# Order of the first and second scores in the second attention of a hybrid block on one Trainium2 core

## The reference, cut to what matters

```python
x = x + linear_attention(layernorm(x))
x = x + experts(layernorm(x))
x = x + softmax_attention(layernorm(x))      # 16 heads of 8 channels
x = x + experts(layernorm(x))

# softmax_attention, the stage of the change
scores = einsum('bhqd,bhkd->bhqk', q, k) / sqrt(8)
attn = softmax(scores, axis=-1)
out = einsum('bhqk,bhkd->bhqd', attn, v)     # then the output projection
```

## Time and profile before

| | us |
|---|---|
| median of 3 runs | 548.59 (548.36 to 549.55) |
| the profiled execution | 548.98 |
| its span in the trace | 547.3 |
| TensorE busy | 513.8 (94%) |
| VectorE busy | 414.6 (76%) |
| ScalarE busy | 340.0 (62%) |
| GpSimd busy | 333.0 (61%) |

### The profile page before, as it was taken

The page is one execution under the profiler, slowest core; times in us unless marked ns, Lnnn a source line. Parts: engine busy times, 40 slices in busy tenths (PEclk is TensorE's granted clock), DMA queues, the critical chain, the costliest instruction groups (busy, mean ns, idle before and its releaser), DMA issues. The chain is left out here.

```text
span 547.3 us, 11826 instructions
## 1 busy us (share of the span) xinstructions
PE 513.8 (94%) x3821; PEld 391.7 (72%) x3821; DVE 414.6 (76%) x1106; ACT 340.0 (62%) x605; POOL 333.0 (61%) x423
## 2 busy tenths in 40 slices
PE   7888989999999999999888998989989999999997
PEld 6665656887888888886645655555878888888885
DVE  4678798798787886677877888898588686776665
ACT  3777765766565556655657676666765656565553
POOL 5897582789767877867233142230577685766563
PEclk9999999999999999999989999999999999999999
DMA  7476870732944233582533444200522444465241
GB/s 177 133 254 207 259 253 3 128 106 79 134 128 128 78 134 99 163 208 65 188 109 98 135 134 138 65 15 4 117 94 100 108 143 123 93 143 128 89 144 37
DMA packets 48566, 67.60 MB, mean 124 GB/s; under 512 B 6641, under 2 KB 18946, under 8 KB 48514
## 3 DMA queue, kind: packets, MB, share of 16 engines
q1 hardware_dynamic: 45408, 66.47, 43.4%
q10 hardware_dynamic: 3106, 0.48, 0.5%
HBM read 53.56 MB, written 13.37 MB: 122 GB/s over the span
## 5 line engine op out<-in xcount | busy, mean ns | idle before, releaser
L789 POOL TENSOR_TENSOR KS<-PT,QS 128x512 fp32r<-128x512 f32 x143 | 185.2, 1296 | 78.7 <-ACT QS L1032 72.1
L1027 ACT ACTIVATE bank<-bank 128x512 f32<-128x512 f32 x128 | 74.6, 583 | 97.5 <-PE bank L1059 96.9
L1773 DVE TENSOR_TENSOR PT<-CS,bank 128x512 f32<-128x512 f32 x128 | 87.6, 685 | 51.0 <-PE bank L1059 49.6
L1057 PE MATMUL bank<-XH,WH 128*128 128x512 f32 (+1 forms) x288 | 115.0, 399 | 0.0
L1059 PE MATMUL bank<-XH,WL 128*128 128x512 f32 (+1 forms) x288 | 112.4, 390 | 0.0
L1058 PE MATMUL bank<-XL,WH 128*128 128x512 f32 (+1 forms) x288 | 112.2, 390 | 0.0
L1032 ACT ACTIVATE QS<-PT 128x512 fp32r<-128x512 f32 x144 | 89.9, 625 | 9.1 <-DVE PT L1778 8.9
L1778 DVE TENSOR_TENSOR PT<-PT,bank 128x512 f32<-128x512 f32 x128 | 88.1, 688 | 8.0
L1659 DVE TENSOR_REDUCE MEXP<-bank 128x4 f32<-128x1024 f32 x64 | 78.2, 1223 | 19.8 <-PE bank L1179 19.3
L931 ACT ACTIVATE PT<-bank 128x1024 f32<-128x1024 f32 x64 | 65.5, 1026 | 37.1 <-PE bank L1213 36.9
L1236 PE MATMUL bank<-PT,V 128*32 128x256 f32 (+1 forms) x1024 | 63.2, 365 | 1.0 <-ACT OTS L945 0.7
(11 more groups left out here) (213 smaller groups left out, 798.3 us busy)
## 6 DMA issues: line engine op xcount, KB each, us to landing
CS<-combine_rows SPq DMA_DIRECT2D x128, 256.0 KB, 3.3
head_rows<-HP SPq DMA_DIRECT2D x28, 256.0 KB, 3.2
QS<-head_rows SPq DMA_DIRECT2D x28, 256.0 KB, 3.0
KS<-head_rows SPq DMA_DIRECT2D x28, 256.0 KB, 3.5
head_rows<-PHI SPq DMA_DIRECT2D x14, 256.0 KB, 4.1
stage<-in_L_ffn_gate_w_dram SPq DMA_DIRECT2D x5, 192.0 KB, 4.1
stage<-in_L_ffn_up_w_dram SPq DMA_DIRECT2D x5, 192.0 KB, 4.3
stage<-in_L_ffn_down_w_dram SPq DMA_DIRECT2D x5, 192.0 KB, 5.5
```

Of the source, the lines that this page charges most:

```text
L789: pool.tensor_tensor(GL[:, (u - 1) % 3, :], GG[:, (u - 1) % 3, :], GH[:, (u - 1) % 3, :].bitcast(f32), ALU.subtract).then_inc(F.gl, 1)
L1027: act.activation(TH[:, u, :] if u < SHARED else G[u % 3][:, :], G[u % 3][:, :], ACT.Silu).then_inc(F.th, 1)
L1057: pe.matmul(out, wh, vh, start=start, stop=False)
L1773: dve.tensor_tensor(ab, CS[:, e % CBUFS, :], U[u % 3][:, :], ALU.mult).then_inc(F.b, 1)
```

## The change

In the slots up to ITEMS + 1 of the second attention, TensorE issues the second scores ahead of the first scores, in both halves of the slot. The instructions, their operands and their waits are the same; nothing is changed on another engine.

```diff
                 elif n < ITEMS + 2:
+                    scores_less_maxima(1, n - 4)
                     scores(0, n - 2)
-                    scores_less_maxima(1, n - 4)
                     maxima(n - 3)
                     output_turn()
                     side_steps()
@@
                     elif g == 6 and c + 1 < CHUNKS:
                         pe.wait_ge(A.px, 2 * c + 4)
                         values(1, c + 1, PJ)
+                    scores_less_maxima(0, n - 4)
                     scores(1, n - 2)
-                    scores_less_maxima(0, n - 4)
                     values_product(n - 5)
```

## The result

Four executions of the changed kernel took 558.49 to 562.39 us, median 560.14; the kernel before took 549.07 beside them (548.36 to 552.70). The ratio is 1.0201 (95% interval 1.0169 to 1.0233), or 11.1 us between the medians. 557.0 was forecast, within 552 to 563.

The account below looks back on a forecast made before the run. A two-burst ring through TensorE, VectorE and ScalarE was taken to bound the second attention. Longer ring intervals 9.0, less 1.2 from long ones, plus 0.6 clock gave +8.4 us on the 548.59 median: 557.0 us, range 552 to 563.

Parts of the forecast that it names:

- What bounds the stage: Second attention: first scores (F), VectorE maximum, second scores (G), ScalarE exponential form a ring of 3.59 us over two bursts.
- A waiting first holds a ready second: TensorE's queue: a G waiting for its maximum holds the F behind it, though that F is released at 1.64 us.
- The interval 2.03: Ring-bound bursts of the second attention: with G first, each burst takes 2.03 us instead of 1.80.
- The lower bound of 1.94: Ring-bound bursts: F only 0.02 behind G and VectorE 0.58 behind F give 1.94 us an interval, 552.2 us in all.
- The ring's part of the sum: Second attention's 58 intervals: 39 short ones add 9.02 us, one adds 0.02, longer ones give back 1.25.
- The exponential leaves the path: ScalarE's exponential in the second attention gets 0.3 us of slack, while the maximum has none.
- Late VectorE side work adds nothing beyond the first line: Where statistics delay a maximum: two intervals take 4.31 us against 4.24, covered by the 39 intervals' +9.02; nothing added.
- The clock, +0.6 for one more fall: TensorE's clock in the second attention: one more fall to 1.2 GHz, priced at the mean of 0.38 and 0.87 us.
- The rival that the clock stays low for half of the stage: Second attention: half of the 58 intervals take about 2.6 us instead of 2.03, 16.5 us more, near 573; 9%.
- no difference: TensorE's queue: F passes the waiting G by using other array rows, pace stays 1.80, 548.6 us; 4%.
- faster: Ring-bound intervals: the exponential starts 0.10 us earlier and each of 39 loses that, 3.9 us, giving 544.7; 4%.

## Why the prediction was right, step by step

- **What bounds the stage** (the ring F, maximum, G, exponential over two bursts, 3.59 us): right. A longer step of either kind lengthens a pair of bursts of the kernel before by about its own length, 3.58 to 3.77 us for 0.20 of maximum and to 3.72 for 0.12 of exponential, so half of it for each burst. The totals are larger; for the exponential most of the excess lies where the clock fell.
- **A waiting first holds a ready second**: right. The F at 317.74 was released 0.40 us earlier.
- **The interval 2.03**: right to 0.02 (2.01 in the undisturbed bursts, mean 2.03 over 38). Its parts were split wrongly: I had F 0.10 behind G and 0.56 to 0.58 to VectorE; it is 0.02 and 0.62, and that the two errors nearly cancel is luck. The 0.10 came from a misreading of the earlier trace rows: I took the G at 310.50 for one that was not itself waiting. It was, for this maximum of the kernel before:
```profile
309.13 1.23 DVE L1659 TENSOR_REDUCE MEXP<-bank 128x4 f32<-128x1024 f32 x1
```
It ends at 310.36, and 0.14 later is 310.50. The lower bound of 1.94 had the right offset, 0.02, with the hand-over of 0.58, and the two do not come together.
- **The ring's part of the sum**, +9.0 - 1.2 = +7.8: right; +8.0 between the two traces with the clock full, and 556.96 against 557.0 - 0.6 = 556.4 in time.
- **The exponential leaves the path**: right, as the longer exponential shows at no cost.
- **Late VectorE side work adds nothing beyond the first line**: roughly right. Behind the statistics the interval was 2.32 where I had 2.28 (F at 326.33 to F at 328.65).
- **The clock, +0.6 for one more fall**: the term that was too small. It measured 3.2 us in the medians. More idle time did come with more falls, but I counted one of the length seen before. The profiled execution, the one with the lowest clock of the four, has five in the stretch where the kernel before has two, and two of them are long, 13.7 us from 279.3 and 10.2 us from 364.7. The rival that the clock stays low for half of the stage was too strong even there: 0.87 on average over 127 us is some 33 us at 0.50 (0.13 x 127 / 0.50).
- **Rivals**: no difference (F slips past) and faster are refuted by the timeline. The row that the *faster* rival leaned on, a maximum 0.5 us early at 329.21, came from ScalarE's side work and was no sample of the ring.

## What to carry to other kernels

When two results share an in-order queue and each waits for another engine, write down the round that each order closes: here two rings of two bursts became one of a single burst, and each burst went from 1.8 to 2.0 us although no instruction was added. In this kernel the member whose partner step is shorter, first in both halves, was 2% faster than second in both; second in the first half alone cost nothing. One of two symmetric swaps can be free where both together are not; try them apart. Idle time put into TensorE cost twice here, once as time (7.9 us) and once as clock (3.2 us).

## What the runs showed of the hardware

- Two groups of four matmuls on different row groups of the array, issued one behind the other when both are free, start 0.02 us apart, and the second's consumer starts 0.62 us behind it (315.71, 315.73, 316.35). The Trainium skill, "TensorE: Matmul & The Clock Gate", Part 3, "The mechanism", has matmuls start in strict program order; here the trace has pairs of the later group start between pairs of the earlier one. Its order does hold at a semaphore: in no burst of the changed kernel did an F start ahead of a waiting G, though the F at 317.74 was free at 317.34.
- The clock fell to 0.50, 1.2 GHz, in a stage in which TensorE was busy 82% and no wait of its in the bursts was longer than 1.0 us; 189 more matmuls in the same stage kept it at 1.00.
- The kernel before ran at clocks from 0.98 to 1.00 from one execution to the next, and its time went with it, 547.4 to 553.7 us.
